# Gate silu as tanh plus two POOL operations, beta added one stage earlier, one statistics instruction later

## The reference

```
# layer 2, coupling: three cycles of a small network (gelu, gelu, gelu,
# sigmoid) that twists x, then
x2 = layernorm(x + coupled(x))

# layer 3, selective scan over the tokens, 16 states per channel
x, z = split(x2 @ w_in.T + b_in)
dt = softplus(x @ w_dt.T + b_dt)
B, C = x @ w_B.T + b_B, x @ w_C.T + b_C
for each token:  h = exp(A*dt)*h + dt*B*x ;  y = sum_n(h*C) + D*x
o  = (y * silu(z)) @ w_out.T + b_out
x3 = layernorm(x2 + layernorm(o + x2)*gamma + beta)

# layer 4
h  = silu((layernorm(x3)*ln_gamma + ln_beta) @ w1 + fc1_bias)
out = layernorm(2*x3 + 0.5*(h @ w2 + fc2_bias))
```

## Time and profile before

| | us |
|---|---|
| three runs | 1147.61, 1148.70, 1149.27 |
| median | 1148.7 |
| the profiled execution | 1148.39 |
| its span | 1146.6 |
| PE busy | 1021.7 (89%) |
| DVE busy | 924.9 (81%) |
| ACT busy | 840.9 (73%) |
| POOL busy | 701.7 (61%) |

### The profile page before, as it was taken

The page is one execution under the profiler, slowest core; times in us unless marked ns, Lnnn a source line. Parts: engine busy times, 40 slices in busy tenths (PEclk is TensorE's granted clock), DMA queues, the critical chain, the costliest instruction groups (busy, mean ns, idle before and its releaser), DMA issues. The chain is left out here.

```text
span 1146.6 us, 17126 instructions
## 1 busy us (share of the span) xinstructions
PE 1021.7 (89%) x5234; PEld 701.9 (61%) x5234; DVE 924.9 (81%) x1166; ACT 840.9 (73%) x1641; POOL 701.7 (61%) x623
## 2 busy tenths in 40 slices
PE   6999999999879999995648699999999999988887
PEld 4777777777643344443436367576676766756576
DVE  7999999999824665453799898999999999999741
ACT  7868878887634456556667789898988989896843
POOL 3466656775721453353666868778697886968420
PEclk9999999999979999998788799999999999999999
DMA  6534443443232011114755455546555675656201
GB/s 184 148 120 134 116 123 112 134 116 114 85 108 78 1 37 44 48 55 107 209 143 166 115 167 129 150 132 156 154 132 168 139 161 137 152 136 140 70 9 37
DMA packets 93230, 133.81 MB, mean 117 GB/s; under 512 B 8786, under 2 KB 47698, under 8 KB 93140
## 3 DMA queue, kind: packets, MB, share of 16 engines
q1 hardware_dynamic: 93140, 132.73, 42.5%
HBM read 116.45 MB, written 14.16 MB: 114 GB/s over the span
## 5 line engine op out<-in xcount | busy, mean ns | idle before, releaser
L2197 DVE TENSOR_TENSOR_SCAN state<-bank_a,h,state 128x512 f32<-128x512 f32 x256 | 316.0, 1269 | 34.0 <-POOL state L2405 12.2
L2405 POOL TENSOR_TENSOR state<-uc,Bb 128x1024 f32<-128x1024 f32 x64 | 151.0, 2369 | 61.7 <-DVE prod L2203 36.6
L2405 POOL TENSOR_TENSOR state<-s,Bb 128x1024 f32<-128x1024 f32 x64 | 151.0, 2369 | 49.4 <-DVE prod L2203 33.6
L1655 PE MATMUL bank_y<-ident,prod 128*128 128x128 f32 x1024 | 139.3, 283 | 30.5 <-DVE prod L2203 30.5
L1655 PEld LDWEIGHTS bank_y<-ident,prod 128*128 128x128 f32 x1024 | 123.9, 147 | 69.0 <-DVE prod L2203 36.9
L2203 DVE TENSOR_TENSOR prod<-state,bank_c 128x1024 f32<-128x1024 f32 x128 | 154.0, 1203 | 6.4 <-ACT bank_c L1876 4.4
L1700 PE MATMUL bank_m<-w,f_h 128*128 128x256 f32 x448 | 104.5, 383 | 0.0
L40 PE MATMUL bank_m<-nT,w 128*128 128x512 f32 x224 | 102.0, 593 | 0.9 <-ACT nT L1938 0.9
L1871 ACT ACTIVATE bank_a<-dtc,A 128x512 f32<-128x512 f32 x128 | 86.6, 682 | 18.0 <-DVE state L2197 14.3
L1871 ACT ACTIVATE bank_a<-s,A 128x512 f32<-128x512 f32 x128 | 86.2, 680 | 11.8 <-DVE state L2197 11.6
L1700 PEld LDWEIGHTS bank_m<-w,f_h 128*128 128x128 f32 x448 | 84.7, 193 | 13.1 <-issue 2.4
(11 more groups left out here) (365 smaller groups left out, 2444.3 us busy)
## 6 DMA issues: line engine op xcount, KB each, us to landing
Bb<-CB_rows SPq DMA_DIRECT2D x128, 256.0 KB, 4.2
Cb<-CB_rows SPq DMA_DIRECT2D x128, 256.0 KB, 4.6
abc<-decays SPq DMA_DIRECT2D x32, 512.0 KB, 4.6
Ebc<-ramps SPq DMA_DIRECT2D x64, 128.0 KB, 3.2
uT<-in_uT SPq DMA_DIRECT2D x8, 512.0 KB, 4.5
u<-in_u SPq DMA_DIRECT2D x8, 512.0 KB, 4.0
x_tokens<-x2s SPq DMA_DIRECT2D x8, 512.0 KB, 2.9
x_rows<-x1T SPq DMA_DIRECT2D x8, 512.0 KB, 2.7
```

Source lines behind the costliest of these rows:

```text
L1655: i = e.matmul(p_y[c // 2][:, at:at + P], prod[n % 2][:, k, c * CH:(c + 1) * CH], ident[:, :], start=False, stop=(n == NS - 1), is_transpo ...
L2197: e.tensor_tensor_scan(s[:, k, :], p_a[k][:, :], s[:, k, :], h0[:, n, k:k + 1], ALU.mult, ALU.add).then_inc(v_s, 1)
L2405: e.tensor_tensor(state[at % 3][:, :, :], uc[b % 2][:, :, :], both(Bb[n % 4][:, :]), ALU.mult).then_inc(p_b, 1)
```

## The change

Three things are changed.

1. Gate. `evac_z` now does two operations on each half of z: the copy into `zg` as before, and a tanh of z/2 into a new tile `zt`. `silu_z` on ACT is gone. POOL gets `gate_silu(cur)` at the place of `shifted`: `zt = 0.5*zt + 0.5` and `zg = zt*zg`, each over 128x1024, the second waiting for the first. It runs for all eight blocks, in the passes 0 to 7.
2. Beta. POOL adds beta in the coupling stage, `with_beta` into `xb`, once for each block. The tokens are stored from `xb`, and the store waits for that. Beta is taken off the output bias, so that `o + x2` stays what it was. `shifted` and `end_shifted` are gone.
3. Statistics. `stats6(old, 0)` moves from behind `scan(post, 10, 0)` to just ahead of `stats6(old, 1)`.

```diff
...
@@ -1066,8 +1069,8 @@
                 for to, what in loaded:
                     e.dma_start(to, what).then_inc(ld, DMAS)
                 for b in range(NB):
-                    e.wait_ge(c_n, 4 * b + 4)
-                    e.dma_start(x2_tokens[:, b * NC:(b + 1) * NC, :], x2s[b % 2][:, :, :]).then_inc(c_tok[b % 2], DMAS)
+                    e.wait_ge(c_xb, b + 1)
+                    e.dma_start(x2_tokens[:, b * NC:(b + 1) * NC, :], xb[b % 2]).then_inc(c_tok[b % 2], DMAS)
                     if b == NB - 2:
                         e.wait_ge(a_bc, 1)
                         e.dma_start(scratch["CB_rows"][:, 0:TB], CB[:, :]).then_inc(st_CB, DMAS)
...
@@ -1232,7 +1235,7 @@
 
                 def normalize(b):
                     e.wait_ge(c_ln, 4 * b + 4)
-                    after(e, c_tok[b % 2], DMAS * (b // 2))
+                    after(e, c_xb, b - 1)
                     after(e, c_bT, 2 * (b - 1))
                     for c in range(NC):
                         e.activation(x2s[b % 2][:, c, :], b_n[c // 2][:, (c % 2) * DM:(c % 2 + 1) * DM], ACT.Identity, bias=nb[:, c:c + 1], scale=rs[:, c:c + 1]).then_inc(c_n, 1)
...
@@ -1267,6 +1270,7 @@
                 def evac_z(p):
                     e.wait_ge(pe_z, p + 1)
                     e.activation(zg[0][:, 2 * p:2 * p + 2, :].rearrange("p c f -> p (c f)"), b_x[p][:, :], ACT.Copy).then_inc(a_z, 1)
+                    e.activation(zt[:, 2 * p:2 * p + 2, :].rearrange("p c f -> p (c f)"), b_x[p][:, :], ACT.Tanh, scale=0.5).then_inc(a_z, 1)
 
                 def global_net(w):
                     if w == 0:
...
@@ -1371,8 +1375,11 @@
                         e.scalar_tensor_tensor(w2[:, :, :], w2[:, :, :], 0.5, s2, ALU.mult, ALU.mult).then_inc(c_w, 1)
                     if w == 10:
                         e.tensor_scalar(bias_f[:, 2 * DM:3 * DM], bias_f[:, 2 * DM:3 * DM], 0.5, None, ALU.mult).then_inc(c_w, 1)
+                        for i in (0, 32):
+                            e.tensor_tensor(bias_f[i:i + 1, DM:2 * DM], bias_f[i:i + 1, DM:2 * DM], bet[i:i + 1, :], ALU.subtract).then_inc(c_wb, 1)
                     if w == 11:
                         e.wait_ge(c_w, 6)
+                        e.wait_ge(c_wb, 2)
                         e.tensor_copy(bias[:, :], bias_f[:, :]).then_inc(c_w, 1)
                         e.tensor_copy(ones_r[:, :], ones[:, :]).then_inc(c_w, 1)
                     if w == 12:
...
@@ -1431,6 +1438,14 @@
                     e.sem_inc(step, 1)
                     e.tensor_scalar(nb[:, :], nb[:, :], -1.0, None, ALU.mult).then_inc(c_ln, 1)
 
+                def with_beta(b):
+                    if b == 0:
+                        e.wait_ge(c_w, 4)
+                    e.wait_ge(c_n, 4 * b + 4)
+                    after(e, c_tok[b % 2], DMAS * (b // 2))
+                    e.sem_inc(step, 1)
+                    e.tensor_tensor(xb[b % 2], x2s[b % 2][:, :, :], bet.rearrange("p (o f) -> p o f", o=1).to_broadcast([P, NC, DM]), ALU.add).then_inc(c_xb, 1)
+
                 def drive():
                     e.wait_ge(a_sp, 1)
                     e.sem_inc(step, 1)
...
@@ -1446,6 +1461,8 @@
                         drive()
                     if ended(w - 3) is not None:
                         norm(ended(w - 3))
+                    if ended(w - 4) is not None:
+                        with_beta(ended(w - 4))
 
             with nc.Block() as block:
                 block.sync(sync)
...
@@ -1609,7 +1626,7 @@
                 def x_proj(b, m):
                     if m == 0:
                         e.wait_ge(ld_xT, DMAS * b)
-                        e.wait_ge(a_z, 2 * b)
+                        e.wait_ge(a_z, 4 * b)
                     else:
                         e.wait_ge(a_x, 2 * b + 1)
                     passes(e, single[:, :], [(w_xz[:, k, m * P:(m + 1) * P], xT[:, k, :]) for k in range(KD)]).then_inc(pe_x, 1)
...
@@ -1904,11 +1921,9 @@
                 def evac_z(b, p):
                     e.wait_ge(pe_z, 2 * b + p + 1)
                     after(e, pe_gt, 2 * (b - 1))
+                    e.wait_ge(p_zs, 2 * b)
                     e.activation(zg[b % 2][:, 2 * p:2 * p + 2, :].rearrange("p c f -> p (c f)"), single[:, :], ACT.Copy).then_inc(a_z, 1)
-
-                def silu_z(b):
-                    e.wait_ge(a_z, 2 * b + 2)
-                    e.activation(zg[b % 2][:, :, :].rearrange("p c f -> p (c f)"), zg[b % 2][:, :, :].rearrange("p c f -> p (c f)"), ACT.Silu).then_inc(a_zs, 1)
+                    e.activation(zt[:, 2 * p:2 * p + 2, :].rearrange("p c f -> p (c f)"), single[:, :], ACT.Tanh, scale=0.5).then_inc(a_z, 1)
 
                 def evac_gated(b, k):
                     after(e, pe_o, 2 * b)
...
@@ -2110,7 +2125,6 @@
                         silu_up(last, 1)
                         silu_up(last, 2)
                     if live(cur):
-                        silu_z(cur)
                         spread_C(cur, 2)
                     if 0 <= last < NB - 2:
                         silu_up(last, 3)
...
@@ -2203,7 +2217,7 @@
                     e.tensor_tensor(prod[n % 2][:, :, :], state[(NS * b + n) % 3][:, :, :], both(p_c[:, :]), ALU.mult).then_inc(v_g, 1)
 
                 def gate(b, p):
-                    e.wait_ge(a_zs, b + 1)
+                    e.wait_ge(p_zs, 2 * b + 2)
                     e.wait_ge(pe_y, NS * b + NS)
                     part = zg[b % 2][:, 2 * p:2 * p + 2, :].rearrange("p c f -> p (c f)")
                     e.tensor_tensor(part, p_y[p][:, :], part, ALU.mult).then_inc(v_gate, 1)
...
@@ -2313,8 +2326,6 @@
                         second(old, 1)
                     if live(post):
                         scan(post, 10, 0)
-                    if 0 <= old < NB - 2:
-                        stats6(old, 0)
                     if live(post):
                         product(post, 9)
                         scan(post, 10, 1)
...
@@ -2352,6 +2363,7 @@
                     if live(cur):
                         product(cur, 1)
                     if 0 <= old < NB - 2:
+                        stats6(old, 0)
                         stats6(old, 1)
                     if 0 <= post < NB - 1:
                         residual(post, 1)
...
@@ -2404,10 +2416,13 @@
                     e.sem_inc(step, 1)
                     e.tensor_tensor(state[at % 3][:, :, :], uc[b % 2][:, :, :], both(Bb[n % 4][:, :]), ALU.mult).then_inc(p_b, 1)
 
-                def shifted(b):
-                    e.wait_ge(v_pre, 2 * b + 2)
-                    e.sem_inc(step, 1)
-                    e.tensor_tensor(x2, x2, rowwise(bet), ALU.add).then_inc(p_xb, 1)
+                def gate_silu(b):
+                    e.wait_ge(a_z, 4 * b + 4)
+                    e.sem_inc(step, 1)
+                    e.tensor_scalar(zt, zt, 0.5, 0.5, ALU.mult, ALU.add).then_inc(p_zs, 1)
+                    e.wait_ge(p_zs, 2 * b + 1)
+                    e.sem_inc(step, 1)
+                    e.tensor_tensor(zg[b % 2], zt, zg[b % 2], ALU.mult).then_inc(p_zs, 1)
 
                 def norm3(b):
                     e.wait_ge(v_l3, 2 * b + 2)
...
@@ -2470,7 +2485,6 @@
 
                 def summed(b):
                     e.wait_ge(p_gam, b + 1)
-                    e.wait_ge(p_xb, b + 1)
                     e.sem_inc(step, 1)
                     e.tensor_tensor(xl, xl, x2, ALU.add).then_inc(p_add, 1)
 
...
@@ -2485,11 +2499,6 @@
                     e.wait_ge(v_e, e_count)
                     e.sem_inc(step, 1)
                     e.tensor_tensor(to, what, mhalf[:, 0:2], ALU.pow).then_inc(done, 1)
-
-                def end_shifted(p):
-                    e.wait_ge(v_pre, 2 * Z + p + 1)
-                    e.sem_inc(step, 1)
-                    e.tensor_tensor(x2[:, half[p], :], x2[:, half[p], :], row_wide(bet), ALU.add).then_inc(p_xb, 1)
 
                 def end_root3(p):
                     end_root(rs3[:, half[p]], ve3[:, half[p]], p + 1, p_l3)
...
@@ -2514,8 +2523,8 @@
                         into(cur, 2)
                         into(cur, 3)
                         into(cur, 4)
-                    if 0 <= post < NB - 1:
-                        shifted(post)
+                    if live(cur):
+                        gate_silu(cur)
                     if 0 <= old < NB - 2:
                         norm6(old)
                     if live(cur):
...
```

More of the change, by code:

```diff
@@ L986, in build @@
         zg = [zgs[:, q, :].rearrange("p (c f) -> p c f", c=NC) for q in (0, 1)]
+        zt = sb("zt", [P, NC, DM])[:, :, :]
         CB = sb("CB", [2 * NS, TB])
@@ L1027, in coupling @@
             c_cs, c_tw, c_o1, c_st, c_gv, c_w = (sem(n) for n in ("cs", "tw", "o1", "st", "gv", "w"))
-            c_o0, c_sx, c_ln, c_pz = (sem(n) for n in ("o0", "sx", "ln", "pz"))
+            c_o0, c_sx, c_ln, c_pz, c_xb = (sem(n) for n in ("o0", "sx", "ln", "pz", "xb"))
+            c_wb = sem("wb")
             ld = sem("ld")
@@ L1053, in dst @@
                 return (oa, ob, oa)[y][b % 4]
```

(14 more changed lines are left out.)

## The result

| | us |
|---|---|
| changed kernel, five runs | 1152.58 to 1154.74, median 1154.43 |
| kernel before, five runs | 1146.68 to 1149.27, median 1148.43 |
| ratio | 1.0051, 95% interval 1.0036 to 1.0066 |
| profiled execution of the changed kernel | 1154.43, span 1152.6 |

The change costs 6.0 us in the medians and 6.0 us between the two profiled spans (1152.6 − 1146.6). The forecast was slower by 8.4, at 1157.0, with a range of 1151 to 1171. So the sign and the range hold, and the size was 2.4 too large.

What follows compares the result with a forecast made beforehand. POOL's unbroken run up to norm45 was taken to bound each pass for 26 of 67.66 us. Passes 6.1, first block −0.5, coupling stage 2.4 and tail 0.4 sum to +8.4, so 1157 us, range 1151 to 1171.

Steps and rivals of the forecast that it cites:

- S: Time of gate_silu's new one-input 128x1024 operation on POOL: taken at 1.1 us, with bounds of 1.0 and 3.7.
- The tanh: ACT's added operation on half 1 of z, last stage: delays the scan, product(1) and into(4) by 0.5 us a pass.
- A pass: Last stage: POOL's added work ahead of into(5), less its 0.91 us pause for ACT's carry, makes each pass 0.87 longer.
- seven passes (it 1 to 7) have the pattern: Last stage: the cost of one pass, norm6 included, was multiplied by seven, 7 × 0.87 = +6.1 us.
- ACT decides: Rival, chance 0.09: slack absorbs POOL's late into operations, ACT's chain gives −0.54 us a pass; kernel 1143 or 1145.8.
- Coupling stage: End of that stage: block 6's token store waits for POOL's beta addition, delaying SP's queue and the barrier by 2.4 us.
- tail: After the passes: both stats6 stand behind the last product, norm6 comes 0.6 later; taken as +0.4 us.
- from below it is 0, if the queue catches up: Lower bound for the end of the coupling stage: no delay if SP's queue catches up, against +2.4 us taken.
- The first block: Last stage, it 0: POOL gets 3.6 us new work, ACT loses a silu and two table loads; taken as −0.5.
- S slow: Rival, chance 0.28: POOL's one-input operation takes 2.36 us, kernel 1167; at 3.7 it is 1178.
- The terms cancel: Rival, chance 0.11: half of the 6.1 absorbed, SP's queue catches up, first block gains; kernel 1148 to 1151 us.
- DVE's scan behind the silus: Expected sign in the last stage's passes: this scan no longer waits for ACT; 1.7 of its 1.80 us pause used.

Runs made afterwards that it cites:

- e8: Kernel before plus an unread tanh on ACT for each half of z in the last stage: 1151.76 us, ratio 1.0029.
- e6: Changed kernel with block 6's B and C rows and their loads ahead of its tokens on SP: 1152.86 us, ratio 1.0036 to before.
- e9: Changed kernel with stats6(old, 0) back at its old place on DVE, ahead of product(post, 9): 1154.41 us, ratio 1.0045 to before.
- e1: Changed kernel without gate_silu's one-input operation, so the gate is no silu: 1146.76 us, ratio 0.9986 to before.
- e2: Changed kernel with a second one-input operation of 128x1024 in gate_silu: 1162.93 us, ratio 1.0129 to before.
- e3: Changed kernel with gate_silu moved on POOL from behind into(4) to behind into(14): 1149.55 us, ratio 1.0008 to before.
- e5: Changed kernel with gate_silu one step earlier on POOL, between into(3) and into(4): 1146.73 us, ratio 0.9985 to before.
- e4: Changed kernel with z's silu back on ACT (no tanh, no gate_silu), beta's move and later statistics kept: 1152.32 us, ratio 1.0024 to before.
- e12: Kernel before with block 6's rows ahead of its tokens and the tanh gate, gate_silu between into(3) and into(4); beta stays in shifted: 1142.63 us, ratio 0.9949.

## Why the prediction was right, and where its size was off

*The mechanism* was right: POOL's work ahead of `into(5)`, less the old pause, plus the delay by the tanh. S was taken at 1.1 and is 1.058, at the lower end of its range; the fill was the right neighbour and the scalings the wrong one. The rule of the Trainium skill (GPSIMD Engine Reference, Engine selection) on one-input and two-input operations fits these two: 1058 and 2360 ns for the same shape, where DVE's product of that shape takes 1203 before the change. The tanh was taken at 0.5 and is 0.45 (e8). A pass was forecast at +0.87 and is +0.72. One label in the prediction is wrong: the matmuls at 861.98 make half 0 of z, and half 1 follows at 882.92, just ahead of the copy at 886.15. The sum does not hang on it, since the same instruction is taken both times.

*The step that failed* is "seven passes (it 1 to 7) have the pattern". `norm6` works on the block three back, so it is on POOL's list only from `it` 3 on. In the second interval of the marks it is missing, POOL has its pause and ACT decides: −0.54 instead of +0.87. The code quoted ahead of the prediction has the condition on `old` in it; my account of the pass took `norm6` for granted. This is 1.4 of the 2.4 us. The pass `it` 1 has no `norm6` either, so by the same step the first interval should be shorter too, which would bring the forecast to 8.4 − 2 × 1.41 = +5.6. But that interval was 1.60 longer in the profiled execution: there PE's eight matmuls of `out_proj` took 3.20 us at 618.53, the same eight 1.89 in the kernel before, and DVE waited for them, at a granted clock of 0.82 against 0.86 between 612 and 660 us. In e6 and e9, whose passes are the changed kernel's, this interval was 67.11 and 66.36, against 66.76 in the kernel before. In both the eight matmuls took 1.89. So the +1.60 is not a price that every execution of these passes pays, and without it the span would show some +4.4 (6.0 − 1.60, an estimate). Nor is it an accident of a rare execution: the profiled one is the median of the changed kernel's five, while those of e6 and e9 are the second lowest and the lowest of theirs.

*Luck.* The granted clock, averaged over an execution, bears on this. Of the 74 runs of the kernel before that stand beside the experiments, the 20 with a clock of 0.965 to 0.967 have a median of 1147.2, the 18 with 0.960 to 0.962 one of 1149.7. The changed kernel's five all lie at 0.960 to 0.962, with a median of 1154.43. At a like clock the change thus costs some 4.7 us (an estimate), and the rest of the 6.0 goes with the clock, for which the prediction had no term. That part moved the measured time toward the forecast without being in it, which is luck. Whether the change lowers the clock or these five runs met it so stays open.

*The last interval* gave +0.27 in this trace where a pass gives +0.72; in e6 and e9 it was 67.38 and 67.33 against 66.67, so +0.71 and +0.66. What was missing belongs to single executions too. Coupling stage (+2.10 for +2.4) and tail (+0.44 for +0.4, e9) came as forecast, and "from below it is 0, if the queue catches up" was 0.3 of 2.4. The first block gave −0.32 for −0.5, but the same stretch took 68.45 us in the kernel before, 68.13 in the changed one, 68.00 in e6 and 67.20 in e9, so a term of this size can't be read from one trace.

*The rivals.* S slow: excluded by the 1.058. ACT decides: false for the passes with `norm6` (e1, e2), true for the pass without it, with the price that was given. The terms cancel: no. Of what I said one would see, one sign was not there: DVE's scan behind the silus still waits for ACT, 0.37.

## What to carry to other kernels

An operation that moves to another engine is free or expensive by the step at which it stands on that engine's list, not by that engine's busy share: against the 67.17 of e1, `gate_silu` cost 1.22 us a pass at one place, 0.48 at a second (e3, by another chain) and 0.04 at a third (e5), one step away. Before a pass is multiplied by seven, read each pass's list for the instructions that its conditions leave out. When a change bundles several edits, time the one with the gain alone: here the tanh gate was worth having and the move of beta paid for nothing (e4, e12).
